# Turning attention probabilities with 32x32 block transposes on VectorE and a trip through DRAM in place of TensorE

## The chip, the cores and the metric

The kernel runs on one core of one Trainium2 chip, as one program launched once. The metric is the device time of that launch in microseconds. Engines are named as the profile names them: PE (TensorE), DVE (VectorE), ACT (ScalarE), POOL (GpSimd) and SP (SyncE, which here only issues DMAs).

## The reference: what is computed

Four transformer layers over x of shape 8 batches x 128 tokens x 512, each layer a gated cross attention to `ctx_4096` (8 x 128 x 512) and then a gated feed-forward part. Layers 0, 1 and 3 have 32 query heads of 128 and 8 key/value heads of 128; layer 2 has small heads of 16 and is not touched here. Cut to what matters (layer 1; layer 0 has rotary positions instead of the two norms, layer 3 is like layer 1):

```python
q = (hidden_states @ q_proj_w.T).reshape(B, Q, 32, 128).transpose(0, 2, 1, 3)
k = (cross_attention_states @ k_proj_w.T).reshape(B, KV, 8, 128).transpose(0, 2, 1, 3)
v = (cross_attention_states @ v_proj_w.T).reshape(B, KV, 8, 128).transpose(0, 2, 1, 3)
q = rmsnorm(q, q_norm_w)
k = rmsnorm(jnp.repeat(k, 4, axis=1), k_norm_w)
scores = jnp.einsum('bhqd,bhkd->bhqk', q, k) * scale + attention_mask
attn = jax.nn.softmax(scores, axis=-1)
out = jnp.einsum('bhqk,bhkd->bhqd', attn, jnp.repeat(v, 4, axis=1))
x = x + tanh(g) * (out.transpose(0, 2, 1, 3).reshape(B, Q, 4096) @ o_proj_w.T)
```

The feed-forward parts are a low-rank mixture over 28 experts (layer 0), a quantised matrix (layer 1), a top-2 mixture of 16 experts (layer 2) and a top-1 mixture of 8 experts (layer 3).

## The kernel before

**Units.** In layers 0, 1 and 3 the attention is cut into 64 units, one for each key/value group g (8) and batch b (8). A unit has R = 4 query heads of 128 queries against 128 keys, so its scores are 128 x 512 values: queries on the partitions, head and key along the free dimension. Every matrix product is made from a high and a low part in fp32r (suffixes `_h` and `_l`): ACT copies the high part, DVE or POOL subtracts it to get the low part, and PE does three matmuls for each product.

**Order.** `Schedule` lays the parts of a unit at steps: `self.at(i, order, name, ...)` puts part `name` at step i and at place `order` inside the step. A unit begins a step; its parts are spread over steps i to i+6, so that seven units are under way at once. Each engine then walks the same sorted list `plan.order` and issues its own instructions for each part, in that order, with semaphore waits in front of them. An engine that waits holds up all that is behind it in its list. The parts of a unit that started at step i:

- i, 70: `keys_values` and `project` (PE, into B_qkv); ACT then copies v_h and, in layers 1 and 3, squares the rest; DVE makes v_l and, in layer 0, three rotary products (L1513, L1517, L1518), in layers 1 and 3 the sums of squares (L1503). POOL finishes the rotary sums (L2095, L2096) or computes the reciprocal roots (L2085, L2088).
- i+1, 10: `normalise` (layers 1 and 3: DVE L1528). i+1, 50: `turn_q` (PE transposes q and k, L807, L809), `split_k`.
- i+2, 40: `scores` (PE L817, L818). i+2, 41: `low_scores` (ACT copies the low scores to S, POOL adds the mask, L2106). i+2, 56: `mask` (DVE adds the high scores, L1557, and takes the row maxima, L1560). i+2, 71: `exp` (ACT writes W[k], L1283), k being the step's parity.
- i+3, 11: `probs` (DVE reciprocals, L1565; POOL multiplies W[k] by them, L2145: `normalise_p`).
- i+4, 30: `turn_p`: PE transposes the four 128 x 128 blocks of W[k] into the PSUM bank B_pt (L827), ACT copies pT_h from it, DVE makes pT_l from it.
- i+5, 20: `times_v` (PE L837), ACT copies oT_h, DVE makes oT_l. i+6, 0: `attn_out` (PE L761 into B_out), DVE adds to X (L1578).

**Weights.** SP loads each 128 x 512 half of a piece of weights into one of two `raw` buffers (`load`), and a `next` event splits it: ACT copies ring_h, then DVE (place 46 of a step) or POOL (places 5, 24 or 90, in steady steps 90 alone) makes ring_l. A group of eight units uses five pieces, ten halves. In layer 0 SP also issues `clear_slots`, 32 fills of 1 MB of `slots_x` in DRAM, at place 47 of every second step.

**What the change touches:** the `turn_p` functions of PE, ACT and DVE (L822, L1288, L1567), the two `split_k` functions (L1195, L1543), `exp` (L1277), `low_scores` (L1266), SP's program and the layout of the masks. S and W are [128, 2, 512] tiles in SBUF, indexed by k.

Of the kernel before, what the change touches and what calls it, by code (L numbers as in the profile page):

```python
# [52 lines left out]
SCALE = float(P) ** -0.5  # L53
KINDS = ("rope", "norm", "plain", "norm")
# [32 lines left out]
class Schedule:  # L87
# [44 lines left out]
    def attention(self, layer, first, base):  # L132
# [3 lines left out]
        for u, (g, b) in enumerate(units):  # L136
# [23 lines left out]
            self.at(i + lag - 2, 46 if first_turn else 30, "turn_p", layer, u)  # L160
# [277 lines left out]
def build(nc, io, out, sublayers=8):  # L438
    with ExitStack() as ctx:
# [145 lines left out]
        slots_y = nc.dram_tensor("slots_y", (TILES2 * P, D), F32).ap()  # L585
        scales = [tables[:, :, :].rearrange("p a n -> p (a n)")[:, h * HALF:(h + 1) * HALF] for h in range(2)]
# [42 lines left out]

        variance, rstd_done, mean_square, rms, roped, probs, pw_made = (  # L630
# [35 lines left out]
        def per_head(ap):  # L666
            return ap.rearrange("p (r k) -> p r k", r=R)

# [76 lines left out]
        def tensor_program(pe):  # L745
# [341 lines left out]
            def tile3(t):  # L1087
# [6 lines left out]
                for c in range(CH):  # L1094
# [8 lines left out]
                     "turn_p": turn_p, "times_v": times_v, "attn_out": output, "low": low, "turn_low": turn_low,  # L1103
# [8 lines left out]
        def scalar_program(act):  # L1112
            v_reader, sq_reader, W_reader, qT_reader, oT_reader, pT_reader, spare_reader = {}, [], {}, [], [], [], []
# [81 lines left out]
            def split_k(layer, u):  # L1195
# [9 lines left out]
                copy(kT[0], B_out[:, 0:P], scale).then_inc(*kT_hi.now((layer, u)))  # L1205
# [27 lines left out]
            def exp2(c):  # L1233
                act.wait_ge(*maxed.of(c))
                if c > 3:
                    act.wait_ge(*p_turned.of(c - 4))
                elif c < 2:
                    for token in W_reader[c]:
                        act.wait_ge(*token)
                for j in range(R):  # L1240
                    t = act.activation(probs2[c % 4][:, cols(j)], scores_bank2(c)[0][:, cols(j)], ACT.Exp,
                                       bias=nmx[:, c % 4, j:j + 1])
# [23 lines left out]
            def low_scores(layer, u):  # L1266
# [125 lines left out]
            def turn3(t):  # L1392
# [3 lines left out]
                elif t == 0:  # L1396
# [6 lines left out]
                     "split": split, "project": project, "turn_q": turn_q, "split_k": split_k, "scores": scores, "low_scores": low_scores, "exp": exp, "turn_p": turn_p, "times_v": times_v, "low": low,  # L1403
# [6 lines left out]
        def vector_program(dve):  # L1410
# [132 lines left out]
            def split_k(layer, u):  # L1543
                kind, g, b, k, vs = unit(layer, u)
                bank = B_out[:, 0:P]
                dve.wait_ge(*kT_hi.of((layer, u)))
                if kind == "rope":
                    sub(kT[1], bank, f32(kT[0])).then_inc(*kT_lo.now((layer, u)))
                else:
                    dve.scalar_tensor_tensor(out=kT[1], in0=bank, scalar=wqk[:, layer // 2:layer // 2 + 1], in1=f32(kT[0]),  # L1550
# [479 lines left out]
            def tile3(t):  # L2030
# [10 lines left out]
                     "probs": denominators, "turn_p": turn_p, "times_v": times_v, "attn_out": output, "low": low,  # L2041
# [204 lines left out]
        def sync_program(sync):  # L2246
# [31 lines left out]

            def fill_tables():
# [32 lines left out]
            parts = {"load": load, "fill_tables": fill_tables, "clear_slots": clear_slots,  # L2312
# [150 lines left out]
```

## Time and profile before

| | |
|---|---|
| median of 3 runs | 2681.81 us (2679.26 to 2682.94) |
| profiled execution, first to last instruction | 2680.3 us, 1.5 us under the median |
| PE busy | 2458.8 us, 92%, 13741 matmuls |
| PE weight loads | 2088.5 us, 78% |
| DVE busy | 1818.8 us, 68% |
| ACT busy | 1264.2 us, 47% |
| POOL busy | 1241.2 us, 46% |
| DMA | 191.67 MB, mean 72 GB/s |

A row of a timeline gives the start, the duration, the engine, the line, the instruction, its output and inputs and the shapes, then in brackets the idle time of the engine before it and what ended that. Durations of PE are modelled and overlap (a matmul of 512 columns is shown with 0.39 us and the next starts 0.23 us after it), and DVE rows overlap by up to 0.1 us too: what an instruction costs is read from start to start. A count x4 merges four equal instructions into one row. All times are in us unless marked ns.

### The profile page before, as it was taken

What the parts mean: (1) busy time and instruction counts of PE and PEld (TensorE: products, weight loads), DVE (VectorE), ACT (ScalarE), POOL (GpSimd) and SP (SyncE); (2) the same over time, 40 slices, a digit from 0 to 9 for tenths busy, and PEclk for the clock granted to TensorE, in tenths of its full rate; (3) what the DMA queues carried; (4) which work ended last, traced back from release to release, by engine and by line L of the source; (5) the groups of instructions that cost most, each with busy time, mean ns of one, the idle gap of its engine ahead of it and who ended that gap; (6) DMA issues with size and microseconds to landing.
All of it is one profiled execution on the core that took longest, in us unless ns stands there. A gap on an engine that the chain in (4) does not pass through costs nothing.

```text
span 2680.3 us, 42144 instructions
## 1 busy us (share of the span) xinstructions
PE 2458.8 (92%) x13741; PEld 2088.5 (78%) x13741; DVE 1818.8 (68%) x3407; ACT 1264.2 (47%) x3698; POOL 1241.2 (46%) x1382
## 2 busy tenths in 40 slices
PE   5899999998889999999987888899689999999977
PEld 4788888887778888888776776676578888888853
DVE  4677777767777777777665776563477777777762
ACT  2455555554246555555533545223245555555520
POOL 4645545554235444444434666423444444444443
PEclk9999999999999999999999999899899999999979
DMA  3112222331112111111100000159501111100154
GB/s 107 63 52 99 84 96 84 103 103 56 48 56 95 40 40 33 34 34 37 60 28 17 1 1 26 67 192 358 177 28 49 34 36 40 40 32 25 41 198 147
DMA packets 67884, 191.67 MB, mean 72 GB/s; under 512 B 10097, under 2 KB 10737, under 8 KB 64730
## 3 DMA queue, kind: packets, MB, share of 16 engines
q1 hardware_dynamic: 51936, 139.85, 15.4%
q0 software_dynamic: 10224, 42.03, 4.5%
q10 hardware_dynamic: 5514, 7.11, 0.8%
q8 instruction: 118, 1.93, 0.3%
q14 instruction: 92, 0.75, 0.1%
HBM read 170.57 MB, written 52.14 MB: 83 GB/s over the span
## 4 chain that ended last, share of the span: by engine, by line
PE 73%; DVE 7%; DMA 6%; POOL 5%; issue 5%; ACT 3%; ACTq 0%; SPq 0%; POOLq 0%; DVEq 0%
PE B_qkv L761 30%; PE B_out L761 19%; PE B_more L837 4%; PE B_s L817 4%; DMA slots_y<-S 3%; PE B_qT L807 3%; PE B_more L827 3%; PE B_s L818 2%; PE B_more L761 1%; DMA out_x<-rows_last 1%; DVE X L1578 1%; PE B_more L911 1%; DVE xn L1461 1%; DMA raw<-in_pieces 1%; PE B_out L809 1%
## 5 line engine op out<-in xcount | busy, mean ns | idle before, releaser
L1283 ACT ACTIVATE W<-S,nmx 128x128 f32<-128x128 f32 x768 | 297.6, 394 | 49.7 <-DVE nmx L1560 49.6
L2085 POOL TENSOR_SCALAR rn<-ss 128x5 f32<-128x5 f32 x128 | 25.5, 199 | 609.7 <-DVE ss L1503 609.7
L1180 ACT ACTIVATE sq<-B_qkv 128x640 f32<-128x640 f32 x127 | 89.6, 706 | 409.1 <-PE B_qkv L761 409.1
L2106 POOL TENSOR_TENSOR S<-S,mask 128x512 f32<-128x512 f32 x192 | 251.4, 1310 | 16.5 <-ACT S L1116 16.3
L1578 DVE SCALAR_TENSOR_TENSOR X<-B_out,gates,X 128x512 f32<-128x512 f32 x200 | 150.3, 751 | 151.7 <-PE B_out L761 151.7
L2145 POOL TENSOR_TENSOR W<-W,rden 128x512 f32<-128x512 f32 x192 | 199.9, 1041 | 88.6 <-DVE rden L1565 88.3
L761 PE MATMUL B_qkv<-ring_h,xnT_h 128*128 128x512 f32 x540 | 215.8, 400 | 9.8 <-DVE spare_l L1412 4.0
L761 PE MATMUL B_out<-ring_h,oT_h 128*128 128x512 f32 x516 | 206.0, 399 | 14.5 <-DVE kT L1550 9.1
L817 PE MATMUL B_s<-kT,qT_h 128*128 128x256 f32 x768 | 204.6, 343 | 12.1 <-DVE xnT_l L1412 9.9
L761 PE MATMUL B_qkv<-ring_l,xnT_h 128*128 128x512 f32 x540 | 214.3, 397 | 0.0
L761 PE MATMUL B_qkv<-ring_h,xnT_l 128*128 128x512 f32 x540 | 212.4, 393 | 0.0
L761 PE MATMUL B_out<-ring_l,oT_h 128*128 128x512 f32 x516 | 206.0, 399 | 0.0
L761 PE MATMUL B_out<-ring_h,oT_l 128*128 128x512 f32 x516 | 203.4, 394 | 0.0
L1412 DVE TENSOR_TENSOR v_l<-B_qkv,v_h 128x128 fp32r<-128x128 f32 x189 | 55.1, 291 | 215.9 <-ACT v_h L1116 215.7
L1116 ACT ACTIVATE oT_h<-B_more 128x512 fp32r<-128x512 f32 x200 | 120.0, 600 | 151.4 <-PE B_more L837 148.3
L2095 POOL TENSOR_TENSOR qk<-sq,qk 128x320 f32<-128x320 f32 x64 | 55.9, 873 | 284.5 <-DVE qk L1518 284.5
L818 PE MATMUL B_s<-kT,qT_l 128*128 128x128 f32 x768 | 172.4, 224 | 0.0
L761 PE MATMUL B_qkv<-ring_h,ctxT_h 128*128 128x256 f32 x540 | 164.1, 304 | 0.0
L2077 POOL TENSOR_TENSOR ring_l<-raw,ring_h 128x512 fp32r<-128x512 f32 x107 | 137.4, 1287 | 47.5 <-ACT ring_h L1116 47.5
L817 PEld LDWEIGHTS B_s<-kT,qT_h 128*128 128x128 f32 x768 | 146.0, 190 | 14.8 <-issue 14.7
L2088 POOL TENSOR_TENSOR rn<-rn,pw 128x5 f32<-128x5 f32 x128 | 151.5, 1184 | 10.6
L1412 DVE TENSOR_TENSOR oT_l<-B_more,oT_h 128x512 fp32r<-128x512 f32 x200 | 133.9, 669 | 31.6 <-ACT oT_h L1116 31.4
(504 smaller groups left out, 7923.5 us busy)
## 6 DMA issues: line engine op xcount, KB each, us to landing
raw<-in_pieces SPq DMA_DIRECT2D x270, 256.0 KB
slots_x<-in_zero SPq DMA_DIRECT2D x32, 1030.0 KB, 6.7
raw<-in_experts SPq DMA_DIRECT2D x16, 768.0 KB, 7.2
w<-in_experts SPq DMA_DIRECT2D x8, 1024.0 KB, 16.8
slots_y<-S SPq DMA_DIRECT2D x31, 256.0 KB
xn<-slots_x ACTq DMA_DIRECT2D x8, 257.5 KB, 6.3
raw<-in_ctxT SPq DMA_DIRECT2D x8, 256.0 KB
X<-in_x ACTq DMA_DIRECT2D x8, 256.0 KB, 2.6
```

The source lines that it names most:

```text
L761: t = pe.matmul(dst, a, b, start=first and n == 0, stop=last and n == len(steps) - 1)
L817: pe.matmul(B_s[:, cols(r, 2 * P)], qT[0][:, cols(r)], kT_both[:, :], start=True, stop=False)
L818: t = pe.matmul(B_s[:, cols(2 * r)], qT[1][:, cols(r)], kT[0], start=False, stop=True)
L837: t = pe.matmul(B_oT[:, :], a[:, vs, :], c[:, :], start=n == 0, stop=n == 2)
L1116: return act.activation(dst, src, ACT.Copy, scale=scale)
L1283: t = act.activation(W[:, k, cols(r)], S[:, k, cols(r)], ACT.Exp, bias=nmx[:, k, r:r + 1], accum_out=den[:, k, r:r + 1])
L1412: return dve.tensor_tensor(dst, a, b, ALU.subtract)
L1578: dve.scalar_tensor_tensor(out=X[:, b, 0:D], in0=bank[:, :], scalar=factor, in1=X[:, b, 0:D], op0=ALU.mult, op1=ALU.add).then_inc(*x_add.n ...
L2077: pool.tensor_tensor(lo, landing_place(item), f32(hi), ALU.subtract).then_inc(*piece_lo["pool"].now(i))
L2088: pool.tensor_tensor(rn[:, k, 0:R + 1], rn[:, k, 0:R + 1], pw[:, 0:R + 1], ALU.pow).then_inc(*rms.now((layer, u)))
L2106: pool.tensor_tensor(S3, S3, m.unsqueeze(1).to_broadcast([P, R, P]), ALU.add).then_inc(*masked.now((layer, u)))
L2145: pool.tensor_tensor(W3, W3, rden[:, k, :].unsqueeze(2).to_broadcast([P, R, P]), ALU.mult).then_inc(*probs.now((layer, u)))
```

## The change

Keys are laid out by block: the masks (on the host) and kT (in `split_k`, by access patterns) hold key 4a + j at column 32j + a. `turn_p` goes; in its place come `blocks_p` (DVE transposes the 32 x 32 blocks of W[k] into S[k]), `store_p` (SP writes S[k] to a DRAM buffer), `load_p` (SP reads it back into W[k] with the partitions regrouped, runs of 128 values) and `split_p` (ACT makes pT_h and DVE pT_l, now both from W[k] in SBUF).

```diff
@@ Schedule.attention
-            self.at(i + lag - 2, 46 if first_turn else 30, "turn_p", layer, u)
+            self.at(i + 3, 31, "blocks_p", layer, u)
+            self.at(i + 3, 32, "store_p", layer, u)
+            self.at(i + 3, 62, "load_p", layer, u)
+            self.at(i + lag - 2, 46 if first_turn else 30, "split_p", layer, u)
@@ build
+        between_p = [nc.dram_tensor(f"between_p{k}", (P * HG,), F32).ap() for k in range(2)]
+        def blocks_first(ap):
+            return ap.rearrange("p (j h q) -> p h j q", j=BLOCKS, q=BLOCK)
+        def by_block(ap):
+            return ap.rearrange("p (i r q) -> p r i q", i=BLOCKS, q=BLOCK)
+        def heads_first(ap):
+            return ap.rearrange("p (r i q) -> p r i q", i=BLOCKS, q=BLOCK)
+        def turned_keys(ap):
+            return ap.rearrange("p (a j) -> p j a", j=BLOCKS)
+        def block_keys(ap):
+            return ap.rearrange("p (j a) -> p j a", j=BLOCKS)
@@ tensor_program
-            def turn_p(layer, u):
-                k = unit(layer, u)[3]
-                pe.wait_ge(*probs.of((layer, u)))
-                bank_free("pt")
-                for r in range(R):
-                    t = pe.transpose(B_pt[:, cols(r)], W[:, k, cols(r)], ident[:, :])
-                t.then_inc(*p_turned.now((layer, u)))
-                read["pt"] = pT_lo.of((layer, u))
@@ scalar_program: split_k
-                copy(kT[0], B_out[:, 0:P], scale).then_inc(*kT_hi.now((layer, u)))
+                copy(block_keys(kT[0]), turned_keys(B_out[:, 0:P]), scale).then_inc(*kT_hi.now((layer, u)))
@@ scalar_program: low_scores
+                elif k in S_reader:
+                    act.wait_ge(*S_reader[k])
@@ scalar_program: exp
-                W_reader[k] = [p_turned.of((layer, u))]
-
-            def turn_p(layer, u):
-                act.wait_ge(*p_turned.of((layer, u)))
+                W_reader[k] = [pT_lo.of((layer, u))]
+                S_reader[k] = p_stored[k].of((layer, u))
+
+            def split_p(layer, u):
+                k = unit(layer, u)[3]
+                act.wait_ge(*p_loaded[k].of((layer, u)))
                 for sem, value in pT_reader:
                     act.wait_ge(sem, value)
-                copy(pT[0][:, :], B_pt[:, :]).then_inc(*pT_hi.now((layer, u)))
+                copy(heads_first(pT[0][:, :]), by_block(W[:, k, :])).then_inc(*pT_hi.now((layer, u)))
@@ vector_program
-            def turn_p(layer, u):
+            def blocks_p(layer, u):
+                k = unit(layer, u)[3]
+                dve.wait_ge(*probs.of((layer, u)))
+                dve.transpose(blocks_first(S[:, k, :]), W[:, k, :].rearrange("p (r j q) -> p r j q", r=R, q=BLOCK)
+                              ).then_inc(*blocks_made.now((layer, u)))
+
+            def split_p(layer, u):
+                k = unit(layer, u)[3]
                 dve.wait_ge(*pT_hi.of((layer, u)))
-                sub(pT[1][:, :], B_pt[:, :], f32(pT[0][:, :])).then_inc(*pT_lo.now((layer, u)))
+                sub(heads_first(pT[1][:, :]), by_block(W[:, k, :]), heads_first(f32(pT[0][:, :]))
+                    ).then_inc(*pT_lo.now((layer, u)))
@@ sync_program
+            def store_p(layer, u):
+                k = unit(layer, u)[3]
+                sync.wait_ge(*blocks_made.of((layer, u)))
+                if p_loaded[k].made:
+                    sync.wait_ge(p_loaded[k].sem, p_loaded[k].by * p_loaded[k].made)
+                sync.dma_start(between_p[k].rearrange("(p n) -> p n", p=P), S[:, k, :]).then_inc(*p_stored[k].now((layer, u)))
+
+            def load_p(layer, u):
+                k = unit(layer, u)[3]
+                sync.wait_ge(*p_stored[k].of((layer, u)))
+                sync.dma_start(W[:, k, :].rearrange("p (i n) -> p i n", i=BLOCKS),
+                               between_p[k].rearrange("(i p n) -> p i n", i=BLOCKS, p=P)).then_inc(*p_loaded[k].now((layer, u)))
...
+        "mask0": _keys_by_block(i["mask_BxSxS2_ik0"].transpose(1, 0, 2)).reshape(P, NB * P),
+        "mask13": _keys_by_block(i["mask_1x1xSxS2_ff0"].reshape(P, P)),
```

DVE's `split_k` takes the same two access patterns as ACT's. Layer 2 keeps its own transposes on PE (`turn_p2`); one wait was added to `exp2` for its first use of S.

## Rows read from the trace of the kernel before

**Rows 1.** Windows: us, then busy of PE, PEld, DVE, ACT, POOL; PEclk; DMA; GB/s
```profile
200.00:600.00 400.00, 399.17 (x2355) 350.30 (x2354) 288.63 (x533) 204.88 (x648) 204.43 (x197) 1.00 0.28 95
850.00:1240.00 390.00, 390.00 (x2308) 342.69 (x2307) 288.23 (x478) 226.25 (x667) 181.99 (x192) 1.00 0.11 35
2050.00:2450.00 400.00, 400.00 (x2361) 351.29 (x2360) 297.39 (x492) 231.74 (x684) 185.78 (x195) 1.00 0.11 36
...
582.00:857.00 275.00, 247.17 (x1382) 211.83 (x1380) 205.16 (x452) 117.79 (x347) 106.30 (x128) 0.96 0.22 74
```
**Rows 2.** Timeline of DVE, one step of layer 0 (to the next X add)
```profile
401.50 0.75 DVE L1578 SCALAR_TENSOR_TENSOR X<-B_out,gates,X 128x512 f32<-128x512 f32 x1 [0.49 <-PE B_out L761]
...
403.43 0.68 DVE L1412 TENSOR_TENSOR pT_l<-B_more,pT_h 128x512 fp32r<-128x512 f32 x1
...
405.51 0.68 DVE L1412 TENSOR_TENSOR qT_l<-B_qT,qT_h 128x512 fp32r<-128x512 f32 x1
...
406.65 0.69 DVE L1557 SCALAR_TENSOR_TENSOR S<-B_s,S 128x512 f32<-128x512 f32 x1 [0.26 <-POOL S L2106]
407.37 0.69 DVE L1560 TENSOR_REDUCE nmx<-S 128x4 f32<-128x512 f32 x1
408.55 0.29 DVE L1412 TENSOR_TENSOR v_l<-B_qkv,v_h 128x128 fp32r<-128x128 f32 x1 [0.50 <-ACT v_h L1116]
...
410.99 0.75 DVE L1578 SCALAR_TENSOR_TENSOR X<-B_out,gates,X 128x512 f32<-128x512 f32 x1 [0.49 <-PE B_out L761]
```
**Rows 3.** Timeline of PE in the same step, around the transposes of W
```profile
401.99 0.60 PE L827 MATMUL B_more<-ident,W 128*128 128x128 f32 x4
402.35 0.36 PE L817 MATMUL B_s<-kT,qT_h 128*128 128x256 f32 x1
...
403.30 0.61 PE L807 MATMUL B_qT<-ident,qk 128*128 128x128 f32 x4
```
**Rows 4.** Timeline of a step of layer 1: ACT, DVE and PE; the last row is a later step's
```profile
1044.64 0.71 ACT L1180 ACTIVATE sq<-B_qkv 128x640 f32<-128x640 f32 x1 [3.32 <-PE B_qkv L761]
...
1048.14 0.82 DVE L1528 TENSOR_TENSOR qk<-B_qkv,rn 128x640 f32<-128x640 f32 x1
...
1049.19 0.61 PE L807 MATMUL B_qT<-ident,qk 128*128 128x128 f32 x4
...
1064.52 0.29 DVE L1412 TENSOR_TENSOR v_l<-B_qkv,v_h 128x128 fp32r<-128x128 f32 x1 [0.69 <-ACT v_h L1116]
```
**Rows 5.** Timeline of POOL in the step of rows 2
```profile
401.93 0.87 POOL L2096 TENSOR_TENSOR qk<-sq,qk 128x320 f32<-128x320 f32 x1
402.75 1.28 POOL L2077 TENSOR_TENSOR ring_lent_l<-raw,ring_lent_h 128x512 fp32r<-128x512 f32 x1
403.99 1.04 POOL L2145 TENSOR_TENSOR W<-W,rden 128x512 f32<-128x512 f32 x1
404.99 1.62 POOL L2106 TENSOR_TENSOR S<-S,mask 128x512 f32<-128x512 f32 x1
```
**Rows 6.** DVE's splits from SBUF by tile raw: duration in ns min/median/max, first and last start
```profile
L1412 DVE TENSOR_TENSOR ring_l<-raw,ring_h x83: 678/1432/1778, 100.7 to 2467.0; 128x512 fp32r<-128x512 f32 x83
```
**Rows 7.** Splits of weights in eight steps, 401.4 to 477.3, by line (L2077 POOL, L1412 DVE)
```profile
L2077 POOL TENSOR_TENSOR ring_lent_l<-raw,ring_lent_h x3: 1277/1282/1282, 402.8 to 431.2; 128x512 fp32r<-128x512 f32 x3
L2077 POOL TENSOR_TENSOR ring_l<-raw,ring_h x2: 1288/1292/1297, 440.7 to 450.2; 128x512 fp32r<-128x512 f32 x2
...
L1412 DVE TENSOR_TENSOR ring_l<-raw,ring_h x3: 924/931/1237, 433.1 to 471.1; 128x512 fp32r<-128x512 f32 x3
L1412 DVE TENSOR_TENSOR ring_lent_l<-raw,ring_lent_h x2: 930/1084/1237, 404.7 to 423.6; 128x512 fp32r<-128x512 f32 x2
```
**Rows 8.** The page's DMA issues: a load of 256 KB, median us to landing last
```profile
X<-in_x ACTq DMA_DIRECT2D x8, 256.0 KB, 2.6
```
**Rows 9.** Tile slots_y: the landing of the 31 stores of S (128 x 512) to DRAM
```profile
DMA to landing us min/median/max: 3.6/3.7/3.7
```
**Rows 10.** ACT's copy of 128 x 512 from SBUF, by tile raw
```profile
L1116 ACT ACTIVATE ring_h<-raw x190: 612/625/657, 54.8 to 2466.3; 128x512 fp32r<-128x512 f32 x190
```

More of the change, by code:

```diff
@@ L53 @@
 SCALE = float(P) ** -0.5
+BLOCK = 32
+BLOCKS = P // BLOCK
 KINDS = ("rope", "norm", "plain", "norm")
@@ L628, in build @@
         onehot_made, slot_made, tabled = (signal(n) for n in ("onehot", "slot", "tabled"))
+        blocks_made = signal("blocks")
+        p_stored, p_loaded = ([signal(f"{n}{k}", 16) for k in range(2)] for n in ("p_stored", "p_loaded"))
         variance, rstd_done, mean_square, rms, roped, probs, pw_made = (
@@ L1102, in tensor_program @@
                      "ln_turn": ln_turn, "keys_values": keys_values, "project": project, "turn_q": turn_q, "scores": scores,
-                     "turn_p": turn_p, "times_v": times_v, "attn_out": output, "low": low, "turn_low": turn_low,
+                     "times_v": times_v, "attn_out": output, "low": low, "turn_low": turn_low,
                      "ffn0": ffn0, "ffn1": ffn1, "route2": route2, "rank2": rank2, "turn2": turn2,
@@ L1239, in exp2 @@
                         act.wait_ge(*token)
+                else:
+                    act.wait_ge(*S_reader[c - 2])
                 for j in range(R):
@@ L1402, in scalar_program @@
                      "load_x": load_x, "late_constants": late_constants, "make_gates": make_gates, "make_constants": make_constants, "ln_turn": ln_turn,
-                     "split": split, "project": project, "turn_q": turn_q, "split_k": split_k, "scores": scores, "low_scores": low_scores, "exp": exp, "turn_p": turn_p, "times_v": times_v, "low": low,
+                     "split": split, "project": project, "turn_q": turn_q, "split_k": split_k, "scores": scores, "low_scores": low_scores, "exp": exp, "split_p": split_p, "times_v": times_v, "low": low,
                      "turn_low": turn_low, "route2": route2, "weigh2": weigh2, "turn2": turn2, "load_rows2": load_rows2, "expand2": expand2,
@@ L1544, in split_k @@
                 kind, g, b, k, vs = unit(layer, u)
-                bank = B_out[:, 0:P]
+                bank = turned_keys(B_out[:, 0:P])
+                hi, lo = (block_keys(m) for m in kT)
                 dve.wait_ge(*kT_hi.of((layer, u)))
                 if kind == "rope":
-                    sub(kT[1], bank, f32(kT[0])).then_inc(*kT_lo.now((layer, u)))
+                    sub(lo, bank, f32(hi)).then_inc(*kT_lo.now((layer, u)))
                 else:
-                    dve.scalar_tensor_tensor(out=kT[1], in0=bank, scalar=wqk[:, layer // 2:layer // 2 + 1], in1=f32(kT[0]),
+                    dve.scalar_tensor_tensor(out=lo, in0=bank, scalar=wqk[:, layer // 2:layer // 2 + 1], in1=f32(hi),
                                              op0=ALU.mult, op1=ALU.subtract).then_inc(*kT_lo.now((layer, u)))
@@ L2040, in vector_program @@
                      "normalise": normalise, "fill_tables": fill_tables, "turn_q": turn_q, "split_k": split_k, "mask": mask,
-                     "probs": denominators, "turn_p": turn_p, "times_v": times_v, "attn_out": output, "low": low,
+                     "probs": denominators, "blocks_p": blocks_p, "split_p": split_p, "times_v": times_v, "attn_out": output, "low": low,
                      "turn_low": turn_low, "ffn0": ffn0, "fill_pick": fill_pick, "ffn1": ffn1, "choose2": choose2, "both2": both2_made,
@@ L2310, in load_weights3 @@
                 sync.dma_start(weight3(e), io["experts"][cols(e), :]).then_inc(*x_in[e].now("w"))
-            parts = {"load": load, "fill_tables": fill_tables, "clear_slots": clear_slots,
+            parts = {"load": load, "store_p": store_p, "load_p": load_p, "fill_tables": fill_tables, "clear_slots": clear_slots,
                      "fill_dispatch2": fill_dispatch2, "load_weights2": load_weights2, "contract2": contract2,
@@ L2317, in sync_program @@
                     parts[name](*args)
-            for done in (*landed, scales_in, cols_in, cleared, *consts2_in, dispatch_in, *y_stored, *scattered, *rows_in, *weight_in, *x_in, *small.values(), *rope_in):
+            for done in (*landed, *p_stored, *p_loaded, scales_in, cols_in, cleared, *consts2_in, dispatch_in, *y_stored, *scattered, *rows_in, *weight_in, *x_in, *small.values(), *rope_in):
                 if done.made:
@@ L2344, in _two, with _keys_by_block @@
     return [w[:, 0:2].reshape(P, PIECE), w[:, 2:4].reshape(P, PIECE)]
+def _keys_by_block(mask):
+    return np.ascontiguousarray(mask.reshape(*mask.shape[:-1], BLOCK, BLOCKS).swapaxes(-1, -2)).reshape(mask.shape)
 def _pad(w):
```

4 lines of the change are left out of this document (1 added, 3 removed).

## The prediction

> **What bounds the kernel now.** I read the windows first, then one step on each engine, then the waits inside it. In the long middle stretches of layers 0, 1 and 3 PE is busy for 399 of 400, 390 of 390 and 400 of 400 us at full granted clock, and DVE for 72% to 74% [rows 1]. One step, from one X add to the next, takes 410.99 - 401.50 = 9.49 us [rows 2], and matmuls come at the same 5.9 a us in all three windows (2355 in 400, 2308 in 390, 2361 in 400 [rows 1]). So these stretches are set by PE. They hold 125 units by the windows; the full stretches reach a little beyond, and I count 50 units of layer 0 and 98 of layers 1 and 3 as steady, which leaves 44 of the 192 where attention overlaps the feed-forward parts. There (582 to 857) PE is busy 90% and DVE 75%, and neither alone is the bound [rows 1].
>
> **What is removed.** The four transposes begin at 401.99 and the scores after them at 402.35 [rows 3]: 0.36 us of PE a unit, 192 x 0.36 = 69 us. Their shown 0.60 us is a modelled, overlapping duration; the distance between starts is what comes off.
>
> **What PE meets next, layers 1 and 3.** The chain from the end of `project` to `turn_q` does not shrink: ACT starts the squares at 1044.64, DVE ends L1528 at 1048.14 + 0.82 = 1048.96, PE starts `turn_q` at 1049.19 [rows 4]. That leaves 0.23 us, some 0.05 of it handing over, so 0.18 is slack, and PE would now come 0.36 earlier. Half of the gain turns into a wait of PE for DVE's qk: 98 x 0.18 = 18 us given back. Bounds: 0 if DVE hands over sooner, 98 x 0.36 = 35 if all is lost.
>
> **What is added on DVE.** (a) `blocks_p`: one instruction over 128x512 values. No row shows a block transpose; the nearest rows, DVE passes of this shape, take 0.68 [rows 2], which I take; one pass is also the lower bound, two passes (1.36) the upper. The Trainium skill (VectorE: DVE Perf Modes, The three transpose paths) gives 311 ns for a 128x128 bf16 block transpose on VectorE; no run here shows that, and an estimate from it that scales with the values is four times 311 ns, 1.24 us, by which the layer 0 and layer 1 and 3 terms would stand near their upper bounds, as in the third rival below. (b) pT_l has the same size, but both its inputs are now in SBUF. The split from SBUF shows what that can cost: 678 ns at best, 1432 at the median [rows 6]. In the step of rows 2 DVE's split started at 404.7 [rows 7] and POOL's mask add beside it took 1.62 [rows 5], so I read it as one waiting for the other. The Trainium skill (SBUF — State Buffer, Who interferes with whom) says that a VectorE instruction with two SBUF inputs and a GpSimd one that reads SBUF exclude each other for a whole instruction; the two durations of rows 6 agree, and without that rule the layer 0 term below would be its lower bound. ACT's copies (0.63 from SBUF [rows 10]) replace equal ones and hide in ACT's idle time; kT's strided copies are small, and I cost them at nothing, 0.1 us if I am wrong, in front of scores that have most of a step to spare.
>
> **Where it lies, layer 0.** The new wait is in front of `blocks_p`: it needs POOL's L2145, and behind it DVE has the weight split, qT_l, kT_l, the scores and maxima, then v_l and the rotary products for which POOL and then PE's `turn_q` wait. Take the step of rows 2, with a split on both POOL and DVE. POOL's split runs to 404.0 [rows 5]; pT_l (wanted at 403.43 [rows 2]) waits for it and ends at 404.6; L2145 follows to 405.6, `blocks_p` to 406.3, the mask add to 406.8, DVE's split to 407.4. From qT_l's start to the maxima's end is 408.06 - 405.51 = 2.55, 0.26 of it a wait [rows 2], so 2.3: DVE is free at 409.7. v_l is wanted at 408.55 - 0.36 = 408.2 [rows 2], so it is 1.5 late. Of that the chain can absorb 0.1: POOL's L2096 ends at 402.80 [rows 5], `turn_q` starts at 403.30 [rows 3], 0.5 less 0.05 less the 0.36. PE stalls 1.4. The same count with POOL's split alone gives 0.3, with DVE's alone 0.2, with none 0. Eight steps from 401.4 hold five splits on each [rows 7], in three steps both (402.8, 431.2, 440.7), in two POOL's alone, in two DVE's alone. Mean: (3 x 1.4 + 2 x 0.3 + 2 x 0.2) / 8 = 0.65, x 50 = 32 us. Lower bound, pT_l waiting for nobody: 0.8 in the three, 0.3 on average, 15 us. Upper, a transpose of two passes: 1.25 on average, 63 us.
>
> **The same in layers 1 and 3.** DVE's wait before v_l is 0.69 even in a step with both splits [rows 4], DVE's split loses there the 0.9 us it now spends waiting behind the mask add (1.43 at the median against 0.68 [rows 6]), and POOL is done earlier. 0.68 plus up to 0.6 for pT_l just fits: 0. With a two-pass transpose 0.45 on average, 44 us.
>
> **The DMAs.** Each unit adds two of 256 KB on SP's queue. The only stores of S take 3.7 [rows 9], a load of this size 2.6 [rows 8]. The loop from one `blocks_p` to the next closes over them: 3.7 + 2.6 + ACT 0.63 + pT_l 0.68 to 1.3 + transpose 0.68 + hand-overs 0.2 = 8.5 to 9.1, against a period of 9.13 to 9.3. It just hides; cover gone, every microsecond is a microsecond of each step. The load's runs are 512 bytes, not 2 KB, and in layer 0 it can queue behind a 1 MB fill, so it may take longer. Behind `load_p`'s wait on SP stands the next weight load, which itself waits for POOL's split in the next step: no cost. The exp and low-score writes to W and S come a step after pT_l and the store: hidden. The Trainium skill (DMA: Bandwidth & Descriptors, Anatomy of one DMA) has about 2.0 us plus bytes at 436 GB/s; the estimate is 2.6 for each of the two, 1.1 less than the stores here, and by it the loop would be 7.4 to 8.0.
>
> **Transitions and ends.** In the 44 other units half the path is PE's and half DVE's: half of the 0.36 is not gained (0.18), half of 0.68 is added (0.34), and 0.15 for pT_l's waits: 0.67 x 44 = 30 us; bounds 0 (all hidden) and 44 x 1.3 = 57. At the end of each of the three layers the trip through DRAM, 6.3 us, lies in steps with little other work: I take half of it, 10 us in all; bounds 0 and 20.
>
> **Sum**: -69 + 18 + 32 + 0 + 30 + 10 = +21 us on the profiled 2680.3, so 2701; the median of the runs stands 1.5 above the profiled span: **2703 us**, 0.8% slower. With all lower bounds it is -69 + 15 = -54, 2628; with all upper ones but the DMA's, -69 + 35 + 63 + 44 + 57 + 20 = +150, 2832. The forecast's own range is 2687 to 2755.
>
> **Rivals.**
> 1. *The gain stays* (ends faster). POOL's normalised W is there before DVE asks, DVE's idle quarter takes the transposes, only the 18 us are given back: 2682 - 69 + 18 = 2631. For it: DVE's 72% and PE's 100% [rows 1]. Against: in three steps of eight of layer 0 `blocks_p` reaches its wait before L2145 can end. It decides if the layer 0 step stays under 9.49. Chance 0.13; half of it kept (2645 to 2676) 0.09.
> 2. *The DRAM loop becomes the bound.* With a load of 4.5 in place of 2.6 the loop is 3.7 + 4.5 + 0.63 + 0.68 + 0.68 + 0.2 = 10.4: 148 x 0.9 = 133, plus some 20 in the other units, 2835. It decides from a store and load of 7.2 together. Chance 0.13.
> 3. *The block transpose takes two passes*: 18 + 63 + 44, then 44 x (0.18 + 0.68 + 0.15) = 44 for the other units, + 10 - 69 = +110, 2792. Nothing in the trace speaks for or against. Chance 0.09.
> 4. *A draw*, gain and stalls cancelling within 0.2% (5.4 us, about what a measurement of this kernel can tell from no change): 0.08.
>
> **How the numbers follow.** The forecast has 0.48. Slower by over 0.2%: 0.48 + 0.13 + 0.09 = 0.70; same 0.08; faster 0.13 + 0.09 = 0.22. The range 2655 to 2800 leaves out the first rival (0.13) and most of the second's upper part (0.07).
>
> **What would show it.** The profile after should have 768 fewer matmuls, 192 transposes on DVE of about 0.68, and 384 more DMAs. Layers 1 and 3: spacing of X adds 9.3, with PE's `turn_q` waiting for DVE's qk. Layer 0: spacing 9.13 without splits and about 10.5 where both engines split, PE waiting for POOL's qk. pT_l should show two durations, 0.68 and over 1. ACT should wait little for the load of W. Wrong if layer 0 runs at 9.2 (first rival), if ACT waits for W in every step (second), if the transposes show 1.3 (third), or if another wait that I do not see, such as that of S for the store, is in the path.

## The result, and the profile after

The changed kernel takes 2720.96 us (median of 4 runs, 2719.18 to 2722.91) against 2681.62 for the kernel before: ratio 1.0142, 95% interval 1.0127 to 1.0157. It is 1.4% slower. The forecast was 2703, 0.8% slower; its sign holds and 18 us are missing. The profiled execution went from 2680.3 to 2721.1 us, +40.8.

The windows of the kernel after, in the order of [rows 1]:
```profile
200.00:600.00 400.00, 379.59 (x2119) 322.93 (x2117) 314.31 (x554) 200.08 (x618) 199.40 (x190) 1.00 0.43 141
850.00:1240.00 390.00, 383.83 (x2151) 330.64 (x2150) 325.76 (x525) 225.93 (x669) 200.97 (x191) 1.00 0.31 98
2050.00:2450.00 400.00, 395.60 (x2226) 341.72 (x2225) 340.94 (x543) 235.31 (x695) 212.00 (x201) 1.00 0.30 95
```
PE was busy for 399 of 400 us in layer 0 [rows 1] and now is for 380; in layers 1 and 3 it was busy all of the time and now is idle for 4 to 6 us. It has less to do in each unit and still waits. The groups and the DMA issues on the page of the kernel after:
```profile
L2140 POOL TENSOR_TENSOR S<-S,mask 128x512 f32<-128x512 f32 x192 | 293.2, 1527 | 46.1 <-ACT S L1134 45.4
...
L1436 DVE TENSOR_TENSOR pT_l<-W,pT_h 128x512 fp32r<-128x512 f32 x192 | 220.9, 1150 | 67.0 <-ACT pT_h L1134 66.5
...
L1596 DVE STREAM_TRANSPOSE S<-W 128x512 f32<-128x512 f32 x192 | 134.7, 702 | 37.0 <-POOL W L2179 37.0
...
between_p<-S SPq DMA_DIRECT2D x192, 256.0 KB, 2.0
W<-between_p SPq DMA_DIRECT2D x192, 256.0 KB, 3.0
slots_x<-in_zero SPq DMA_DIRECT2D x32, 1030.0 KB, 6.2
...
w<-in_experts SPq DMA_DIRECT2D x8, 1024.0 KB, 13.3
```
The block transpose is one pass, 702 ns. pT_l went to 1150 ns from the 0.68 us of [rows 2]. Store and load of a unit's probabilities land in 2.0 and 3.0 us, 5.0 together, where the prediction had 6.3. Yet ACT waits for that load, by the waits of the whole kernel after, then of 200 to 600 us, then of 850 to 1240 us (us in total, times, longest):
```profile
ACT pT_h L1134 <- DMA W<-between_p: 71.0, 39, 12.9
```
```profile
ACT pT_h L1134 <- DMA W<-between_p: 41.0, 22, 3.2
```
```profile
PEld B_qT L834 <- DVE qk L1552: 10.0, 39, 0.3
ACT pT_h L1134 <- DMA W<-between_p: 6.8, 5, 2.8
```
More than half of it is in layer 0, where about every second step has one; one single wait of 12.9 us stands elsewhere. The fills run on to 872 us, into layer 1. Both kinds of wait have the same shape, and SP's queue shows it. Here are SP and then ACT of the kernel after, in layer 0:
```profile
432.19 0.32 SPq L2318 DMA_DIRECT2D between_p<-S  x1
432.56 0.49 SPq L2332 DMA_DIRECT2D slots_x<-in_zero  x1
434.25 0.37 SPq L2323 DMA_DIRECT2D W<-between_p  x1
441.23 0.32 SPq L2318 DMA_DIRECT2D between_p<-S  x1
...
443.25 0.37 SPq L2323 DMA_DIRECT2D W<-between_p  x1
```
```profile
439.23 0.63 ACT L1134 ACTIVATE pT_h<-W 128x512 fp32r<-128x512 f32 x1 [1.42 <-DMA W<-between_p]
447.33 0.62 ACT L1134 ACTIVATE pT_h<-W 128x512 fp32r<-128x512 f32 x1
```
Between store and load of the first unit SP issued a 1 MB fill of slots_x. The load, issued at 434.25, was in only at 439.2, 5.0 us later, and pT_h and all behind it on DVE shifted. The next unit's load, 443.25, had no fill ahead of it and was there when pT_h came at 447.33. The step is a mild one of its kind: in the whole trace 30 loads follow right on a fill and land in 4.6 to 8.1 us, median 5.9, the others in 2.5 to 5.1, median 2.9, and 29 of ACT's 39 waits are for one of those 30. And the end of layer 3, SP and then ACT:
```profile
2576.38 5.19 SPq L2357 DMA_DIRECT2D w<-in_experts  x8
2587.52 0.33 SPq L2318 DMA_DIRECT2D between_p<-S  x1
2602.14 0.38 SPq L2323 DMA_DIRECT2D W<-between_p  x1
```
```profile
2604.82 0.63 ACT L1134 ACTIVATE pT_h<-W 128x512 fp32r<-128x512 f32 x1 [12.93 <-DMA W<-between_p]
```
Eight 1 MB expert tiles were issued from 11 us ahead of a 256 KB store. The load can go only when the store has landed: 14.6 us, not 2.0.

Where the 40.8 us are: I take the start of POOL's normalisation of each unit's W (L2145 before, L2179 after, in layer 2 L2137 and L2171; all 224 are in both traces) and subtract. Unit numbers count all 224, with layer 2's 32 in between.

| stretch | difference it adds | forecast for it |
|---|---|---|
| start to unit 5, and last unit to the end | +4.9 and +12.1 = +17.0 | +10 |
| units 5 to 56, layer 0 | +19.3 | -18 + 32 = +14 |
| units 80 to 112 and 168 to 216, layers 1 and 3 | -3.7 - 6.0 = -9.7 | -35 + 18 = -17 |
| the rest | +3.5 + 8.6 + 2.1 = +14.2 | 44 x (0.67 - 0.36) = +14 |
| sum | +40.8 | +21 |

The columns match only roughly: the forecast's 10 us are for the ends of three layers, two of which lie in "the rest", and "the rest" also has 18 units that the forecast counts as steady in layers 1 and 3.

### The profile page after: what moved, and what is told of

It is laid out like the page before. It is cut to its first block, busy times and chain, and to the rows that moved or that the text cites. A ratio compares the mean times of both kernels' runs of the same rounds, so it can differ in the third digit from the quotient of the medians.

```text
span 2721.1 us, 41374 instructions
## 1 busy us (share of the span) xinstructions
PE 2434.1 (89%) x12973; PEld 2033.6 (75%) x12973; DVE 1979.9 (73%) x3599; ACT 1264.7 (46%) x3698; POOL 1300.7 (48%) x1382
## 4 chain that ended last, share of the span: by engine, by line
PE 37%; DVE 19%; POOL 16%; DMA 13%; issue 10%; ACT 4%; DVEq 0%; ACTq 0%; SPq 0%; POOLq 0%
PE B_qkv L788 22%; DMA W<-between_p 5%; POOL rn L2122 5%; PE B_out L788 4%; DVE qk L1552 3%; DVE ss L1527 3%; DMA slots_y<-S 3%; PE B_qT L834 3%; DMA between_p<-S 2%; PE B_more L788 1%; DVE S L1596 1%; POOL ring_l L2111 1%; POOL W L2179 1%; DMA out_x<-rows_last 1%; ACT v_h L1134 1%
## 5 line engine op out<-in xcount | busy, mean ns | idle before, releaser
L2140 POOL TENSOR_TENSOR S<-S,mask 128x512 f32<-128x512 f32 x192 | 293.2, 1527 | 46.1 <-ACT S L1134 45.4
L1436 DVE TENSOR_TENSOR pT_l<-W,pT_h 128x512 fp32r<-128x512 f32 x192 | 220.9, 1150 | 67.0 <-ACT pT_h L1134 66.5
L2179 POOL TENSOR_TENSOR W<-W,rden 128x512 f32<-128x512 f32 x192 | 211.3, 1101 | 97.2 <-DVE rden L1590 97.1
L788 PE MATMUL B_qkv<-ring_h,xnT_h 128*128 128x512 f32 x540 | 216.4, 401 | 10.5 <-DVE spare_l L1436 4.0
L844 PE MATMUL B_s<-kT,qT_h 128*128 128x256 f32 x768 | 192.3, 328 | 14.7 <-DVE xnT_l L1436 12.5
L834 PE MATMUL B_qT<-ident,qk 128*128 128x128 f32 x768 | 127.5, 290 | 43.9 <-DVE qk L1552 18.2
L1596 DVE STREAM_TRANSPOSE S<-W 128x512 f32<-128x512 f32 x192 | 134.7, 702 | 37.0 <-POOL W L2179 37.0
```

Of the source, the lines that this page charges most:

```text
L788: t = pe.matmul(dst, a, b, start=first and n == 0, stop=last and n == len(steps) - 1)
L834: pe.transpose(B_qT[:, cols(h)], qk[:, cols(h)], ident[:, :])
L844: pe.matmul(B_s[:, cols(r, 2 * P)], qT[0][:, cols(r)], kT_both[:, :], start=True, stop=False)
L1436: return dve.tensor_tensor(dst, a, b, ALU.subtract)
L1596: dve.transpose(blocks_first(S[:, k, :]), W[:, k, :].rearrange("p (r j q) -> p r j q", r=R, q=BLOCK)).then_inc(*blocks_made.now((layer, u)))
L2140: pool.tensor_tensor(S3, S3, m.unsqueeze(1).to_broadcast([P, R, P]), ALU.add).then_inc(*masked.now((layer, u)))
```

## The experiments

All times are medians; the ratio is to the kernel before on the same chip, with its 95% interval. The experiments ran on four chips, on which the kernel before has medians from 2679.7 to 2682.3 us, so differences between runs of a few us are rough; where it matters the ratios are compared too. First a ladder: take the change apart from the bottom.

**No turning on either engine.** PE's transposes stay out, and so do DVE's and the DMAs; pT_h and pT_l read W as it is.
```
-            self.at(i + 3, 31, "blocks_p", layer, u)
-            self.at(i + 3, 32, "store_p", layer, u)
-            self.at(i + 3, 62, "load_p", layer, u)
...
-                act.wait_ge(*p_loaded[k].of((layer, u)))
+                act.wait_ge(*probs.of((layer, u)))
```


> This kernel leaves the turning out: no transposes on either engine and no trip through DRAM, pT_h and pT_l are split from W as it stands. Theory A (the cost lies in what was added, and TensorE's 0.36 us a unit is a real gain): 2682 - 69, of which the chain through DVE's qk gives back 12 in layers 1 and 3 (they run at 9.37 a unit in the changed kernel) and pT_l's waits for GpSimd some 5 to 10 in layer 0: 2630 to 2640 us. Theory B (pT_l with two SBUF inputs, which wait for GpSimd, is itself what costs): pT_l is unchanged here, so about 2710.

Measured: 2661.61 us, ratio 0.9931 (0.9914 to 0.9948), 20 us less, between the two expectations. All that TensorE gives back when its 192 transposes go, with pT_l already reading two arrays in SBUF, is 20 of the 69 us. pT_l's mean is already 1188 ns in this run. By the starts on POOL, layer 0's unit takes 9.15 to 9.21 us in place of 9.49 from unit 8 to 48, but those of layers 1 and 3 9.37: 0.12 of the 0.36. In the windows PE is no longer full there (the second row; [rows 1] has 390.00):
```profile
200.00:600.00 400.00, 396.21 (x2257) 345.18 (x2256) 328.38 (x547) 210.20 (x662) 227.66 (x204) 1.00 0.28 95
850.00:1240.00 390.00, 385.44 (x2170) 332.94 (x2169) 321.80 (x484) 227.90 (x677) 204.45 (x194) 1.00 0.11 36
```

**The block transposes, without the trip through DRAM.** pT_h waits for the transpose and reads W.
```
-            self.at(i + 3, 32, "store_p", layer, u)
-            self.at(i + 3, 62, "load_p", layer, u)
...
-                act.wait_ge(*p_loaded[k].of((layer, u)))
+                act.wait_ge(*blocks_made.of((layer, u)))
```


> The block transposes stay, the trip through DRAM is left out (pT is split from W, so the order of the values is wrong). Theory A with its two causes in layer 0: the steps of the changed kernel whose load was in time are spaced 10.12 (both engines split weights), 9.56 (GpSimd alone) and 9.07; over eight steps 9.6, against 9.87 with the trip: 50 x 0.27 = 13 us less, and 5 to 10 less at the ends of the layers: about 2700. Theory C (DVE's occupancy and wait alone cost, the trip is hidden): 2721, as the changed kernel. Theory D (the trip is all of the loss): 2640.

Measured: 2686.51 us, ratio 1.0021 (1.0010 to 1.0032). The 192 transposes on DVE cost 25 us over the run before, and the trip that is left out is worth 34 more in the changed kernel. The time lies below A's and far above D's. The trip through DRAM, costed at nothing in the steady stretches, is the larger part.

**The fills of slots_x moved to layer 2.** SP's other work in layer 0 changes, nothing else.
```
-                self.at(16 + 2 * n, 47, "clear_slots", n)
+                self.at(self.first[2] + 8 + n, 47, "clear_slots", n)
```


> The changed kernel with SP's 32 fills of 1 MB moved from layer 0 to layer 2. Theory A (every second load of W in layer 0 lands late behind a fill, and the step with it is stretched): layer 0 falls from 9.87 a unit to 9.6, 13 us less: about 2708. Theory C (the late loads are hidden): 2721.

Measured: 2702.37 us, ratio 1.0072 (1.0053 to 1.0092): 19 us back. In layer 0 it keeps step with the run without any trip (both +8.9 or +8.8 us on the kernel before at unit 56, where the changed kernel is at +24.2). ACT's waits for W, in this kernel's trace by tile between_p, fall from 39 to 4, and the longest landing stays, that of the store behind the expert tiles:
```profile
  ACT pT_h L1134: 16.2, 4
busy tenths in 40 slices 0000000000000000000000000000000000000000
DMA to landing us min/median/max: 2.0/2.5/15.5
```

**The same fills moved in the kernel before**, as a control.

> The kernel before with the same 32 fills of slots_x moved from layer 0 to layer 2, as the control for the run that moved them in the changed kernel. Theory Q (the fills cost only because the load of the turned probabilities stands behind them on SP's queue): no such load exists here, so no change, 2679 to 2685 us. Theory F (a 1 MB fill costs layer 0 anyway, by its traffic or by delaying weight pieces): some 0.6 us for each of 32 fills, as in the changed kernel, so about 2663 us.

Measured: 2682.37 us, ratio 0.9996 (0.9980 to 1.0012). Q holds: the fills themselves cost layer 0 nothing. Its window has the same PE time and the same count of matmuls as [rows 1], with less than half of the DMA share:
```profile
200.00:600.00 400.00, 399.19 (x2355) 350.32 (x2354) 288.41 (x532) 204.39 (x644) 204.20 (x197) 1.00 0.12 38
```
They cost only once a load that something waits for stands behind them. Whether that load waits for its turn on SP's queue or shares the DMA engines with the fill is not separated here: no run issued the fills, or the trip, from another engine.

**The expert tiles behind the last trip.**
```
-            self.at(self.first[3] + G * NB, 95, "load_weights3", e)
+            self.at(self.first[3] + G * NB + 2, 63, "load_weights3", e)
```


> The changed kernel with one thing moved: the issue of the eight 1 MB expert tiles w<-in_experts, which stood on SP's queue ahead of the last but one unit's load of the turned probabilities in layer 3, now stands behind the last unit's. Theory Q (the trip through DRAM of that unit waits behind the burst: its store was issued at 2587.5 us, its load only at 2602.1, and ACT's pT_h waited 12.9 us for it): that wait under 1 us, the end some 10 to 13 us earlier, 2708 to 2711 us. Theory L (the tiles are then late for the last stage, which begins some 30 us later): the gain is lost to a wait of PE for w, 2718 us or more.

Measured: 2715.05 us, ratio 1.0133 (1.0116 to 1.0150), runs from 2703.42 to 2718.04. The wait went, but for the time the expectation of either theory is only half met: the gain is 6 us by the medians, not 10 to 13, and by the ratios (1.0133 against 1.0142, with intervals that overlap) it is not clear of noise. The profiled execution, the quickest of the five, has 121.2 us from the last unit to the end, against 129.9 for the changed kernel and 117.7 before; the others have no trace. So this run alone would not carry the point. The next one does.

**Both long transfers out of the way.** Fills in layer 2, tiles behind the last trip, the order of the transposes as in the change.

> The changed kernel with both of the long transfers out of the way of the trip through DRAM (the fills of slots_x in layer 2, the expert tiles behind the last trip), and with the order of the transposes as in the change. Theory Q (the trip costs only where it queues behind a long transfer): 2688 to 2693 us, within 6 us of the run that had the transposes but no DMAs (2686.5 us), ACT's waits for W under 10 us in all. Theory W (the trip has a price of its own in each unit, or the expert tiles' delay costs what the wait did): 2698 us or more.

Measured: 2690.56 us (2688.25 to 2692.93), ratio 1.0039 (1.0025 to 1.0053). With the tiles moved it is 12 us below the run with the fills moved alone (9 by the ratios), and from the last unit to the end its trace has 120.5 us in place of 130.7. It is 4 us above the run without DMAs, no more than the intervals of the two allow for noise: in both traces a unit of layer 0 takes 9.51 us (units 16 to 56). All 192 trips still happen. By tile between_p:
```profile
  ACT pT_h L1134: 3.6, 7
busy tenths in 40 slices 0000000000000000000000000000000000000000
DMA to landing us min/median/max: 2.0/2.8/5.1
```
Q holds. The ladder is complete: 2661.6 with nothing turned, +25 for the transposes, +4, within the noise, for the trip where its way is free, +9 to +12 for the expert burst, +19 for the fills.

**pT_l with one input.** Both pT_l and the transposes weigh on DVE; this run takes the second SBUF input away. The fills are moved here too:
```
-                sub(heads_first(pT[1][:, :]), by_block(W[:, k, :]), heads_first(f32(pT[0][:, :]))
-                    ).then_inc(*pT_lo.now((layer, u)))
+                dve.tensor_reduce(pT[1][:, :], W[:, k, :].unsqueeze(2), AX, ALU.max).then_inc(*pT_lo.now((layer, u)))
```


> The changed kernel with the fills moved (2702.4 us), and with pT_l no longer the difference of two arrays in SBUF but a maximum over one element of W alone (one input; it leaves out the subtraction, so the low part of the probabilities is wrong). Theory T (two SBUF inputs make pT_l wait for POOL: mean 1.15 us against 0.68 before, and layer 0's steps with both splits take 10.12 against 9.5): pT_l near 0.7 us, layer 0's spacing 9.2 to 9.4, in all 2685 to 2692 us. Theory O (what costs is the transposes' own 0.70 us on DVE, wherever pT_l stands): 2700 to 2705 us.

Measured: 2681.90 us, ratio 1.0005 (0.9989 to 1.0022), 20 us below the same kernel with two inputs. Theory T. In this kernel's groups, POOL's instruction beside it is shorter as well:
```profile
L2139 POOL TENSOR_TENSOR S<-S,mask 128x512 f32<-128x512 f32 x192 | 241.5, 1258 | 12.2 <-ACT S L1134 10.3
...
L1602 DVE TENSOR_REDUCE pT_l<-W 128x512 fp32r<-128x512 f32 x192 | 129.9, 676 | 17.1 <-ACT pT_h L1134 16.8
```
1150 (1206 with the fills moved alone) became 676 ns on DVE and 1527 (1548) became 1258 ns on POOL, though nothing of POOL's work was touched. The two engines were in each other's way. The Trainium skill (SBUF — State Buffer, Who interferes with whom) has the rule: a VectorE instruction whose two inputs are both in SBUF contends with a GpSimd instruction that reads SBUF, one with at most one such input, outside the modes that use both ports, does not. The two rows agree. Layer 0's unit falls from a mean of 9.51 to 9.31 us (units 16 to 56), and layers 1 and 3 stay at 9.37. The 20 us are no part of the transposes' 25: the run with nothing turned had the same slow pT_l, and its unit of layer 0 took 9.22 us. The slow pT_l without transposes gives 9.22, the transposes without it 9.31, both together 9.51. If the two simply added up, a kernel with neither would take 9.02, less than the 9.07 of the quickest kind of step in these traces, so each seems to cost more beside the other. That is an estimate: the kernel with neither was not run.

**Every transpose done twice in a row**, 0.70 us more of DVE in each unit.
```
+                for last in (False, True):
+                    if last:
+                        dve.wait_ge(once.sem, once.made)
...
+                    t.then_inc(*(blocks_made if last else once).now((layer, u)))
```


> The changed kernel with every one of the 192 groups of transposes done twice in a row (0.70 us more of DVE's time in each unit, 134 us in all; the result is the same). Theory A (DVE's time costs only where a step has no room: layer 0 and the transitions; layers 1 and 3 still have idle time ahead of pT_l): layer 0's spacing +0.6, layers 1 and 3 within +0.1, in all +35 to +50, 2756 to 2771 us. Theory B (the whole 0.70 us stands on the loop in every layer): +0.7 a unit, 2850 us. Theory N (DVE never binds): 2721 us.

Measured: 2754.00 us, ratio 1.0280 (1.0251 to 1.0309), +33 for 134 us of work, a little under theory A's +35. Units 5 to 56 take 23 us more than in the changed kernel; those of layers 1 and 3 take 9.38 against 9.37. There DVE has room for a second transpose whole.

**The transposes later in the step, with the load at place 92.**
```
+            self.at(i + 3, 54, "blocks_p", layer, u)
+            self.at(i + 3, 55, "store_p", layer, u)
+            self.at(i + 3, 92, "load_p", layer, u)
+            self.at(i + lag - 2, 51, "split_p", layer, u)
```


> The changed kernel with another order: blocks_p after DVE's qT_l and kT_l (place 54 in place of 31), the store at 55, the load at 92, split_p at 51 of the next step in place of 30. Nothing is removed. Theory A (DVE stood waiting for GpSimd's W in front of blocks_p, and for late loads in front of pT_l, with qT_l, kT_l and the scores behind it): both waits go, layer 0 runs at 9.2 to 9.4, layers 1 and 3 stay at 9.37: 2721 - 28 and some in the transitions: 2670 to 2695. Theory C (DVE's added work itself is on the path, wherever it stands): 2721, no change.

Measured: 2895.93 us, ratio 1.0812 (1.0773 to 1.0852). Both expectations missed, by 175 us and more. SP of this kernel, and ACT:
```profile
999.84 0.32 SPq L2318 DMA_DIRECT2D between_p<-S  x1
1005.52 0.33 SPq L2311 DMA_DIRECT2D raw<-in_pieces  x1
1005.90 0.43 SPq L2323 DMA_DIRECT2D W<-between_p  x1
```
```profile
1009.66 0.63 ACT L1134 ACTIVATE pT_h<-W 128x512 fp32r<-128x512 f32 x1 [2.71 <-DMA W<-between_p]
```
The store was issued at 999.84 and would land in 2 us, but the load comes at 1005.90, right behind a weight load that SP itself holds back until its buffer is free. I had put the load behind place 90. It costs ACT 280.2 us in 103 waits over the kernel, and a unit 10.3 to 11.2 us. The theory about DVE's order was not tested by it at all, so it was tried again:

**The same order with the load at place 66**, and the fills moved.

> The changed kernel with the fills moved, the transposes placed behind the projection's work on DVE (place 54 in place of 31), the store behind them (55), the load at 66, ahead of the weight load of place 90, and split_p at 51. The run that had the load at 92 stood at 2896 us. Theory A (that run failed only because its load stood behind a weight load on SP's queue; the order of the transposes on DVE itself is better late, since X's addition and the turning of q and k are no longer behind them): ACT's pT_h waits under 0.3 us for W, 2680 to 2695 us. Theory C (the order on DVE is indifferent): 2702 us, as with the fills moved alone. Theory L (a late transpose leaves the trip through DRAM too little time, wherever the load stands): over 2750 us.

Measured: 2692.70 us, ratio 1.0053 (1.0033 to 1.0072): 10 us below the run with the fills moved alone, in the upper part of theory A's range. By the ratios it is only 5 us, and the intervals overlap; the next run shows the gain of the order more surely. pT_l, now beside other work of POOL, has a mean of 858 ns in place of 1206:
```profile
L1436 DVE TENSOR_TENSOR pT_l<-W,pT_h 128x512 fp32r<-128x512 f32 x192 | 164.8, 858 | 14.1 <-ACT pT_h L1134 14.1
```
At its last unit this kernel is 1.7 us ahead of the kernel before; it then loses 14 us behind the expert tiles, where ACT waits 15.9 us at once.

**All three together**: late transposes, fills in layer 2, tiles behind the last trip.

> Three things together: the fills of slots_x moved to layer 2, the transposes late in their step (the order of the run that stood at 2692.7 us) and the expert tiles behind the last trip through DRAM. Theory Q: that order was 1.7 us ahead of the kernel before at the last unit's probabilities and lost 14 us behind them, all of it to the expert burst; without it 2678 to 2682 us, level with the kernel before. Theory L (tiles late): 2690 us or more.

Measured: 2682.18 us (12 runs), ratio 1.0006 (0.9996 to 1.0016). Q holds. Against the run with both transfers moved and the order as in the change (1.0039) the late order is worth 8 us (9 by the ratios), and the intervals do not meet. This is the best whole version of the change that I have, and it is level with the kernel before, not better. Its profiled execution, 4.8 us longer than that of the kernel before, is 11 us ahead over the steady stretches of the table above and loses 16 outside them, at the start, in the transitions and at the end; what loses them there was not taken apart.

**turn_q behind the next projection**, on top of all three, to see whether the 9.37 us can be broken.
```
-            self.at(i + 1, 50, "turn_q", layer, u)
-            self.at(i + 1, 50, "split_k", layer, u)
+            self.at(i + 1, 72, "turn_q", layer, u)
+            self.at(i + 1, 72, "split_k", layer, u)
```


> As the run with all three, and PE's turn_q, with the evictions behind it, moved from place 50 to 72, behind the projection of the next unit. Theory P (the 9.37 us that layers 1 and 3 take in every variant so far is PE's own 9.1 us and the 0.2 to 0.3 us that its turn_q waits for DVE's qk): spacing 9.1 to 9.2 in layers 1 and 3, some 20 to 25 us less, 2655 to 2660 us. Theory R (the loop through qT and the scores sets the 9.37): the wait goes over to the scores, no gain or a loss, 2678 to 2720 us.

Measured: 3681.31 us, ratio 1.3732 (1.3711 to 1.3753). P's hope fell, and R's range as well. The waits of the whole kernel:
```profile
DVE X L1612 <- PE B_out L788: 923.1, 188, 5.6
...
PE B_out L788 <- DVE kT L1575: 455.7, 121, 7.9
```
`turn_q` writes k's transpose into B_out, the bank that `attn_out` fills at the start of each step. Put late, it makes the next `attn_out` wait until DVE has read kT from it. That is a cost of a shared bank, and the run cannot decide between P and R.

## Why the prediction was right, and where it was 18 us short

**Removed, and layers 1 and 3: right, slightly too good.** 0.36 us a unit was to come off PE, and PE then meets DVE's qk, as forecast: 39 waits of 0.26 us in the second window above. The spacing was to be 9.3 and is 9.37, so a third of the gain stays and not half. The stretches counted give -9.7 us for 80 units, -12 for the forecast's 98, against -17. That DVE's extra work costs nothing there is shown, by the run with the transposes doubled. The step in question, kernel after, on POOL, DVE and PE:
```profile
1026.30 1.18 POOL L2122 TENSOR_TENSOR rn<-rn,pw 128x5 f32<-128x5 f32 x1
```
```profile
1026.75 0.75 DVE L1612 SCALAR_TENSOR_TENSOR X<-B_out,gates,X 128x512 f32<-128x512 f32 x1 [0.83 <-PE B_out L788]
1027.51 0.82 DVE L1552 TENSOR_TENSOR qk<-B_qkv,rn 128x640 f32<-128x640 f32 x1
```
```profile
1019.02 0.66 PE L834 MATMUL B_qT<-ident,qk 128*128 128x128 f32 x4
...
1026.33 0.39 PE L788 MATMUL B_out<-ring_h,oT_l 128*128 128x512 f32 x1
...
1028.39 0.66 PE L834 MATMUL B_qT<-ident,qk 128*128 128x128 f32 x4
```
The same place in the kernel before, for [rows 4]:
```profile
1046.96 0.39 PE L761 MATMUL B_out<-ring_h,oT_l 128*128 128x512 f32 x1
```
```profile
1047.39 0.75 DVE L1578 SCALAR_TENSOR_TENSOR X<-B_out,gates,X 128x512 f32<-128x512 f32 x1 [0.82 <-PE B_out L761]
```
qk stands right behind the X add and ends at 1028.33, and `turn_q` starts at 1028.39. So the 9.37 us are a closed loop: 7.31 us on PE from one `turn_q` to the last matmul of `attn_out`, then 2.06 us through the X add and qk to the next `turn_q`. Before, these were 7.26 and 2.23 (medians of 42 steps). From that last matmul to the end of qk it is 2.00 us in both kernels; what the change gains is the slack behind it, 0.17 us (the prediction had 0.18), less some 0.04 because `turn_q` now lasts 0.52 us to the next matmul in place of 0.47. Those are the 0.12. The prediction named the chain through the squares for this; POOL's roots end at 1027.48, 0.03 us before qk starts, so that chain and the one through the X add are equally long, and shortening one alone would give little. PE's own work between `attn_out` and the last scores shrank by 0.43 us and not 0.36 (2.16 to 1.73), and the quickest steps of layer 0 run at 9.08 and not 9.13: this part of the sum was a little small.

**The block transpose: right.** 702 ns for 0.68. The third rival (two passes) is out, and so is the estimate of 1.24 us from the figure for bf16 of the Trainium skill (VectorE: DVE Perf Modes, The three transpose paths).

**pT_l waits for POOL: right in kind.** 1150 ns at the mean, inside the 0.68 to 1.3; taken away, with the transposes in place, it gives 20 us back. In the steps of layers 1 and 3 one sees it at full length, the mask add of POOL beside it long as well; DVE, then POOL, kernel after:
```profile
1019.55 1.36 DVE L1436 TENSOR_TENSOR pT_l<-W,pT_h 128x512 fp32r<-128x512 f32 x1
1020.83 0.70 DVE L1596 STREAM_TRANSPOSE S<-W 128x512 f32<-128x512 f32 x1
```
```profile
1019.32 1.04 POOL L2179 TENSOR_TENSOR W<-W,rden 128x512 f32<-128x512 f32 x1
1020.32 1.74 POOL L2140 TENSOR_TENSOR S<-S,mask 128x512 f32<-128x512 f32 x1
```

**Layer 0: the sum nearly right, by two errors.** The mean stall was to be 0.65 us, with 0.3 as its lower bound. With the fills out of the way it is 9.51 - 9.13 = 0.38 over units 16 to 56; steps with splits on both engines take 9.65 us (ten of seventeen between 200 and 600 us) or 10.12 (six) and not 10.5. The changed kernel has 9.86 - 9.13 = 0.73 there, since 0.35 a unit of queueing came on top, of which the sum held nothing.

**The DMAs: here the prediction failed.** "It just hides" was true of the loop's own length. The store took 2.0 and not 3.7, the load 3.0 and not 2.6, and where its way is free the trip costs some 4 us in all, within the noise. The Trainium skill (DMA: Bandwidth & Descriptors, Anatomy of one DMA) fits its formula on DMAs that GpSimd issues, and these are issued by SP. The estimate from it, 2.6 for each, was above the store and below the load, and its sum of 5.2 nearer to the 5.0 measured than the prediction's 6.3. But the sentence "in layer 0 it can queue behind a 1 MB fill, so it may take longer" was priced at nothing, although the fills' period could be read from the code: one in every second step, between this unit's store and its load. It measured 19 us. The eight expert tiles at the end of layer 3, which the prediction didn't name, measured 9 to 12; they are most of why start and end came to 17 us and not 10. Those two are 28 to 31 us that the sum lacked, and the 0.27 a unit too much in layer 0 hid 13 of them: that the forecast was only 18 us off is in part luck.

**load_p's wait on SP.** "Behind `load_p`'s wait on SP stands the next weight load: no cost" looked at one side. What stands ahead of `load_p` matters more: put behind a weight load that SP holds back, it brought the kernel to 2896 us, where with the load ahead of it (and the fills moved) it takes 2693.

**The other units: about right.** +14.2 for +14, though the units counted are not quite the same, it is one number for three transitions, and I have not taken it apart.

**The rivals.** The gain did not stay: even without any turning it is 20 us. The DRAM loop did not become the bound in the sense of the second rival, with each step a little longer; it failed in single steps. The nearest thing to a draw is what the change could have been with its order settled, 2682.

What stays open: the loop of 9.37 us in layers 1 and 3 is read from the traces. It is the same with no transposes, with them, and with them doubled (9.36 to 9.39), so it is neither DVE's load nor the trip, but no run here shortened the way through the X add and qk. The tiles moved alone gave 6 us by the medians and, with the fills moved too, 12; in the traces the stretch from the last unit to the end became 8.7 and 10.2 us shorter, so the difference between the two may be noise.

## What to carry to other kernels

A small DMA that something waits for must be priced by what its queue has ahead of it, not by its own landing time: list every large transfer issued between its store and its load, and every issue that the queue's engine can be held at, and move those first. Before moving work off a full engine, ask what it meets when it comes sooner; here 0.12 of 0.36 us a unit was there to be had in two layers of three, before the other engine had done anything. A subtraction that read PSUM and SBUF and comes to read SBUF twice is a change of its own, worth 20 us here beside the transposes it came with.

## What the runs showed of the hardware

- A 256 KB store took 2.0 us to land, and 14.6 us when issued behind eight 1 MB loads of the same queue; the 30 loads of 256 KB issued right behind a 1 MB fill took 4.6 to 8.1, median 5.9, the others 2.5 to 5.1, median 2.9.
- 128x512 fp32 values in 32x32 blocks are turned in 702 ns on DVE, against 670 to 690 for plain passes of this size, with the output written in a permuted order.
- A DVE subtraction with both inputs in SBUF took 1206 ns at the mean where a one-input pass of the same size took 676, and POOL's 1.26 us instruction beside it took 1.55. Its place in the step changed the mean to 858.
